# Retrieval feed-forward, state-space stage and eight-head context attention of a decoder joined into one block

## The reference

```
# L2 feed-forward: retrieval of experts beside a dense MLP
q = (x @ Wq.T).reshape(b, t, 2, 4, 64)             # two halves, 4 heads
sim = einsum('pbthn,hkpn->pbthk', q, keys)         # 128 keys
sx, ix = top_k(sim[0], 8); sy, iy = top_k(sim[1], 8)
scores, pk = top_k(all 64 sums of sx and sy, 8)    # per head
indices = ix * 128 + iy at pk                      # beyond 4095: the last row
w = silu(einsum(x, down_embed[indices])) * softmax(scores)
out = (silu(x @ Wg.T) * (x @ Wu.T)) @ Wd.T + einsum(w, up_embed[indices])
# L3 first part: state-space stage
u, v = split(x @ in_proj_w + in_proj_b); v = dwconv3(silu(v))
h[t] = a * h[t-1] + ssm_b * v[t];  y = ssm_c * h + ssm_d * v
out = layernorm((u * silu(y)) @ out_proj_w + out_proj_b + x) * ln_w + ln_b
# L3 second part: 8 heads of 64 over the context
out = softmax(q @ k.T / 8) @ v @ Wo + bo
```

## Time and profile before

| what | us |
|---|---|
| median of 3 runs | 3112.78 |
| lowest and highest run | 3108.11, 3117.63 |
| profiled execution, span from first to last instruction | 3106.5 |
| PE busy | 2320.2 (75%) |
| DVE busy | 1607.0 (52%) |
| ACT busy | 963.3 (31%) |
| POOL busy | 787.0 (25%) |
| mean granted clock of PE, share of full | 0.885 |

### The profile page before, as it was taken

How to read it: one execution, slowest core, us unless ns; L and a number is a source line. 1 busy time by engine, 2 the same in 40 slices (tenths; PEclk the granted TensorE clock), 3 DMA queues, 4 the chain that set the end, 5 groups by cost and what they waited for, 6 DMA issues and landing times. The chain is left out here.

```text
span 3106.5 us, 37880 instructions
## 1 busy us (share of the span) xinstructions
PE 2320.2 (75%) x13729; PEld 1493.0 (48%) x13729; DVE 1607.0 (52%) x4352; ACT 963.3 (31%) x1784; POOL 787.0 (25%) x755
## 2 busy tenths in 40 slices
PE   6877699888777655485677674877777877689786
PEld 3544378735443432462244333666666664237332
DVE  3754300067545657246374666655665544533486
ACT  0132222210241322132114463443334334424343
POOL 1000200041001006451000004777777771000000
PEclk9999699989998877796899897988889889899898
DMA  7200244337006142553500106222222221000000
GB/s 183 63 21 2 99 149 172 143 85 177 11 18 176 38 159 108 182 179 128 94 5 23 69 1 152 66 55 56 53 55 58 62 53 37 0 29 1 1 0 27
DMA packets 126828, 232.20 MB, mean 75 GB/s; under 512 B 38777, under 2 KB 76537, under 8 KB 122560
## 3 DMA queue, kind: packets, MB, share of 16 engines
q1 hardware_dynamic: 73552, 125.12, 14.2%
q0 software_dynamic: 51952, 100.65, 11.0%
q10 hardware_dynamic: 1152, 4.19, 0.3%
HBM read 245.59 MB, written 66.72 MB: 101 GB/s over the span
## 5 line engine op out<-in xcount | busy, mean ns | idle before, releaser
L3192 POOL DMA_INDIRECT L2f_G<-in_L2f_table,L2f_idx x512 | 523.7, 1023 | 288.7 <-issue 155.2
L3249 PE MATMUL psum<-L2f_G,L2f_diag 128*128 128x256 f32 x1024 | 304.4, 463 | 168.8 <-ACT L2f_diag L3319 168.8
L3249 PEld LDWEIGHTS psum<-L2f_G,L2f_diag 128*128 128x128 f32 x1024 | 235.9, 236 | 234.8 <-ACT L2f_diag L3319 192.0
L3427 DVE CUSTOM_DVE_ANT_0 L2f_junk<-L2f_G,L2f_X 128x256 bf16<-128x256 f32 x512 | 182.8, 421 | 254.0 <-DMA L2f_G<-in_L2f_table,L2f_idx 253.9
L3319 ACT ACTIVATE L2f_diag<-const,L2f_actd 128x128 f32<-128x128 f32 x528 | 161.1, 388 | 24.2 <-DVE L2f_actd L3441 24.2
L1191 PE MATMUL psum<-constb 128*128 128x256 bf16 x512 | 81.0, 282 | 96.8 <-ACT L1a_PT L1358 24.6
L2669 POOL DMA_INDIRECT picks_x<-L1f_rows,L1f_put x64 | 71.0, 1109 | 242.1 <-ACT L1f_rows L2759 223.2
L3226 PE MATMUL psum<-xT,L2f_mw 128*128 128x256 f32 x512 | 123.2, 385 | 0.0
L3312 ACT ACTIVATE L2f_actd<-L2f_dots 128x9 f32<-128x9 f32 (+1 forms) x64 | 13.5, 211 | 316.3 <-DVE L2f_dots L3427 316.3
L1358 ACT ACTIVATE L1a_PT<-psum 128x1536 f32<-128x1536 f32 x32 | 46.4, 1450 | 205.5 <-PE psum L1326 205.5
L1191 PEld LDWEIGHTS psum<-constb 128*128 128x128 bf16 x512 | 41.0, 99 | 142.2 <-ACT L1a_PT L1358 32.9
(11 more groups left out here) (689 smaller groups left out, 4882.8 us busy)
## 6 DMA issues: line engine op xcount, KB each, us to landing
L1f_we<-in_L1f_w SPq DMA_DIRECT2D x32, 384.0 KB, 8.2
picks_x<-zeros SPq DMA_DIRECT2D x16, 544.0 KB, 9.1
L1f_xe<-picks_x SPq DMA_DIRECT2D x32, 272.0 KB, 2.9
picks_y<-zeros SPq DMA_DIRECT2D x16, 512.0 KB, 6.4
L2f_G<-in_L2f_table,L2f_idx POOLq DMA_INDIRECT x512, 2.8
slots_x<-zeros POOLq DMA_DIRECT2D x8, 512.0 KB, 7.6
L1f_wb<-in_L2x_w SPq DMA_DIRECT2D x1, 4096.0 KB, 12.2
L1f_g<-picks_y ACTq DMA_DIRECT2D x8, 512.0 KB, 11.9
```

The source lines that it names most:

```text
L3192: nc.gpsimd.indirect_dma_start(out=G[:, h, k, :], out_offset=None, in_=ins["L2f_table"], in_offset=bass.IndirectOffsetOnAxis(ap=IDX[:, t, ...
L3249: mm = nc.tensor.matmul(ps[:, MIX_BANK + t % 2, 0:D], diag[:, i % 2, k, :], row[:, D:2 * D], start=(h == 0 and k == 0), stop=(h == HEADS - ...
L3427: e = V.tensor_tensor_reduce(out=junk[:, k, :], in0=row[:, 0:D], in1=X[:, t % 3, :], scale=1.0, scalar=0.0, op0=ALU.mult, op1=ALU.add, acc ...
```

## The change

Three stages become one block, `peer_tail_stage`. Batch m (256 tokens) goes through the state-space part in the eight steps after its last gather step, and through the context attention in the eight after those. The loop has 81 steps: 64 with gathers and 17 behind them. Chunks of the dense part become 256 tokens, so that a batch is complete after 8 steps. Each of the three parts gets PSUM banks of its own, and so one bank for `up` and one for the picks. The gathered rows lie in a ring of 28. The three normalizations are done a batch at a time, and no table set is named for ACT in this block. L3x's weights are laid in the free columns of both weight buffers. L3f's weights come in two loads once the gather steps are over. A few index instructions of DVE are merged.

```diff
+    CW = SEQ
+    PER = STEPS // B
+    LATER = 2 * PER + 1
+    END = LATER + PER * (B - 1) + PER
+    ROWS = 28
+    MIX, SIM, UP, DOWN, SSM, SSM2, CROSS, CROSS2 = range(8)
+        def ssm_at(i):
+            m, d = divmod(i - PER - 1, PER)
+            return (m, d) if 0 <= m < B else (0, None)
+        def cross_at(i, part):
+            m, e = divmod(i - LATER, PER)
+            return (m, 2 * e + part) if 0 <= m < B else (0, None)
...
+                        if n >= ROWS and (k == 0 or (n - ROWS) % TOPK == 0):
+                            pool.wait_ge(s["pk_used"].sem, s["pk_used"].at((n - ROWS) // TOPK + 1))
+                        nc.gpsimd.indirect_dma_start(
+                            out=G[:, n % ROWS, :], out_offset=None, in_=ins["L2f_table"],
...
@@ PE
-                    if i + 1 < STEPS:
-                        up(i + 1)
-                    if h == 0 and t + 2 < NT:
-                        queries(t + 2)
-                    picks(i)
-                    if i:
-                        down(i - 1)
+                    cross(i, 0)
+                    if h == 0 and 0 < t <= NT:
+                        turn_back(t - 1)
+                    if i < STEPS:
+                        if h == 1 and t + 2 < NT:
+                            pe.wait_ge(s["pk_hid"].sem, s["pk_hid"].at(i + 1))
+                            pe.wait_ge(s["pk_yadd"].sem, s["pk_yadd"].at(t))
+                            similar(t + 2)
+                        if h == 2 and t + 3 < NT:
+                            pe.wait_ge(s["pk_hid"].sem, s["pk_hid"].at(i + 1))
+                            queries(t + 3)
+                    ssm(i)
+                    if i < STEPS:
+                        picks(i)
+                    cross(i, 1)
+                    if i < STEPS:
+                        pe.wait_ge(s["pk_hid"].sem, s["pk_hid"].at(i + 1))
+                        down(i)
...
+                        if i + 1 < STEPS:
+                            up(i + 1)
@@ ACT
+                def inverse_root(bank, root, square, done):
+                    link(nc.scalar.activation(root, ps[:, bank, 0:CW], ACT.Ln, bias=c.eps))
+                    link(nc.scalar.activation(root, root, ACT.Exp, scale=-0.5))
+                    nc.scalar.activation(square, root, ACT.Square).then_inc(s[done].sem, 1)
...
+                    if h == 0 and 0 < t <= NT:
+                        keep(t - 1)
+                    if i < STEPS:
+                        weigh(i)
+                        diagonal(i)
+                    cross(i, 0)
...
+                    ssm(i)
+                    cross(i, 1)
+                    if i < STEPS and h == 3 and t + 2 < NT:
+                        exps(t + 2)
                     if i + 1 < STEPS:
                         gate(i + 1)
@@ DVE
-                    dot(i)
...
-                    gated(i)
-                    weighted(i)
+                    if i < STEPS:
+                        gated(i)
+                    ssm_gate(i)
+                    if i < STEPS:
+                        dot(i)
+                    late = cross_at(i, 0)[1] == 10
+                    if not late:
+                        cross(i, 0)
+                    if i < STEPS:
+                        weighted(i)
...
+                    ssm(i)
+                    if i < STEPS:
+                        if h == 2 and t + 2 < NT:
+                            best_keys(t + 2)
+                        if h == 3 and t + 2 < NT:
+                            best_pairs(t + 2)
+                        if h == 0 and 0 < t < NT - 1:
+                            experts(t + 1)
+                        if i == 1:
+                            prepare()
+                    cross(i, 1)
```

More of the change, by code:

```diff
@@ L82 @@
 }
+ROUTE_N, SSM_N, CROSS_N = PACK["L2f"][1], PACK["L3a"][1], 2 * 2 * 512
+LAST_N = PACK["L3f"][0]["w2"][0]
+CROSS_PLACE = {k: (0, ROUTE_N + a, n) if a < CROSS_N else (1, SSM_N + a - CROSS_N, n) for k, (a, n) in PACK["L3x"][0].items()}
+WIDTHS = (max(PACK["L3f"][1], ROUTE_N + CROSS_N), max(SSM_N + PACK["L3x"][1] - CROSS_N, PACK["L1a"][1], PACK["L1f"][1]))
 CONST, CONST_N = columns(("ident", P), ("mean", P), ("cos", SEQ), ("sin", SEQ), ("eps", 1), ("blank", 16))
@@ L1809, in fixed_ffn_stage @@
         with nc.Block() as block:
-            @block.sync
-            def _(sp):
-                c.prefetch(sp, name)
             @block.gpsimd
@@ L3214, in similar @@
                         for half in range(2):
-                            rows = slice(half * RD, (half + 1) * RD)
-                            mm = nc.tensor.matmul(ps[:, SIM_BANK + half, tile(o_)], q[rows, o_, :],
-                                                  w["keys"][rows, o_ * KEYS:(o_ + 1) * KEYS], start=True, stop=True)
+                            part = slice(half * RD, (half + 1) * RD)
+                            mm = mm_(ps[:, SIM + half, tile(o_)], q[part, o_, :],
+                                     w["keys"][part, o_ * KEYS:(o_ + 1) * KEYS], start=True, stop=True)
@@ L3255, in turn_back, with average @@
                     for j in range(DH):
-                        mm = nc.tensor.transpose(ps[:, MIX_BANK + t % 2, tile(j)], mix[:, 0, tile(j)], c.ident)
+                        mm = nc.tensor.transpose(ps[:, SIM, tile(j)], mix[:, tile(j)], c.ident)
                     mm.then_inc(s["pk_yturn"].sem, 1)
-                c.wait_weights(pe, name)
+                def average(bank, y):
+                    for j in range(DH):
+                        mm = mm_(ps[:, bank, 0:CW], c.mean, y[:, j, :], start=(j == 0), stop=(j == DH - 1))
+                    return mm
@@ L3260, in _ @@
+                c.wait_weights(pe, "L2f")
                 for t in range(2):
@@ L3328, in _ @@
+                c.wait_weights(act, "L3a")
+                nc.scalar.activation(decay[:, :], wa["la"], ACT.Sigmoid).then_inc(s["decay"].sem, 1)
                 for t in range(2):
@@ L3458, in _ @@
                     experts(t)
-                for i in range(STEPS):
+                for i in range(END):
                     t, h = divmod(i, HEADS)
-                    dot(i)
-                    if h == 1 and t:
+                    if i < STEPS:
[8 more added lines that the diff above has]
+                        weighted(i)
+                    if late:
+                        cross(i, 0)
+                    if h == 0 and 0 < t <= NT:
                         add_mix(t - 1)
@@ L3479, in peer_stage @@
         s["even_landed"].base += 16
-        work.close()
-        norm_stage(nc, c, name, acc)
-OTHER = {"L2f": peer_stage, "L1f": moe_top4_stage, "L2x": bitnet_stage, "L0f": moe_top1_stage, "L3f": fixed_ffn_stage, "L3a": ssm_stage}
+OTHER = {"L2f": peer_tail_stage, "L1f": moe_top4_stage, "L2x": bitnet_stage, "L0f": moe_top1_stage, "L3f": fixed_ffn_stage}
 def program(nc, ins, out):
@@ L3518, in program @@
         run = STAGES
-        packed = [n for n in run if n in PACK]
+        packed = [n for n in STAGES if n in PACK and n != "L3f"] + ["L3a"]
         c.w, order = {}, {}
```

966 lines of the change are left out of this document (438 added, 528 removed).

## The result

The changed kernel takes 3329.31 us (median of 4 runs, 3315.74 to 3331.43) against 3114.17 (3108.11 to 3117.63): ratio 1.068, 95% interval 1.066 to 1.071. It is slower by 215 us; the forecast was 3286 with a range of 3185 to 3370. The profiled execution took 3331.43, its span 3329.5, where the earlier trace rows has 3106.5.

A forecast was written before the change was run, and what follows sets the result against it. Gathers on POOL bound the old stage; the new order closes a ring. First picks, query tile, steps (117.6, 123.2, 822.5), tail 109 and end make 1222.3 against 1049.1, 173 more: 3280 span, 3286 us forecast, range 3185 to 3370.

The forecast's parts named there:

- The bound of before: Old retrieval feed-forward: POOL bound it, gathers back to back, one every 1.33 us, 10.6 us per step of eight.
- the closed ring: Gather steps: dots, diagonals, picks, down, up, silu, product wait in a circle, without overlap of the next step; 13.9 us.
- The bare step: Gather step without state-space or attention work, steps 1 to 8: 14.7 us.
- rival B: Lower TensorE clock on all picks: 147 us at most, some 100 to 110 more, 3390 us; chance 0.11.
- The exps of a tile's fourth step: Two table loads around the softmax exp, between picks and next silu in each fourth step, cost some 0.3 us on average.
- The slots: Added state-space and attention work, eight slots each: together 23.1 us per eight steps, 2.9 a step, making 17.5 us.
- the turning point: Mean gather step below which joining the stages pays: 14.1 us, with the bare ring at 13.4 to 14.7.
- Table loads: ScalarE in the joined block: two loads for each Ln with its Exp, some 160 loads in all.
- Rival A: One table load for Ln and Exp, 48 pairs of 1.28 us: 61 us less, 3225 us; chance 0.14.
- The tail: 17 steps after the last gather step: state-space chain about 40, woven attention 28, last attention 41; sum 109 us.
- The last attention's 41: Final attention running alone at the block's end, from Q projection through output and normalization: 41 us.
- Rival C: Gather steps not set by the ring but by the larger of POOL's and PE's work: 124 us less, 2989; chance 0.04.

The follow-up runs named there:

- experiment 1: Changed kernel with the table set holding both Ln and Exp asked for by name on ScalarE: 3271.08 us, ratio 1.051 to the kernel before.
- Experiment 8: Changed kernel with dots ahead of the product, Ln/Exp table set named, up projection ahead of picks in half the steps: 3094.48 us, 0.994.
- experiment 9: Experiment 8 plus four useless TensorE products before the picks in the two middle steps of each tile: 3113.88 us, 1.000.
- 11: Experiment 8 plus four useless TensorE products after each piece of attention work in the 17 steps behind the last gather step: 3102.72 us, 0.997.

## Why the forecast was right, and where its sizes were off

- **The bound of before and the closed ring: right.** Gathers back to back are gone, the ring's five waits show, and opening it by one order on DVE takes 145 us off.
- **The bare step: right but for the picks.** Over steps 1 to 8 the time between two groups of picks is 9.45 us, and the forecast has 9.14 + 0.16 + 0.3 = 9.6. The picks take 6.02 where it has 4.76 + 0.3. So the term "PE idles longer ahead of its picks, for which I add 0.3" is the whole miss of 0.8: it should have been 1.25. Some 0.15 of that are the ninth row's two passes, which the sum has on DVE and ACT but not on PE; the rest is the clock. Over all steps the picks take 5.43 against 4.86 before. That is rival B in part. Against it I had read in the earlier trace rows that the level comes back within one group; it does, but in the bare steps PE idled 3.4 to 6.7 us right before each group, and 6.02 lies two thirds of the way from 3.53 (all passes at 2.4 GHz) to 7.06 (all at 1.2). Filled, the step is 13.69.
- **The exps of a tile's fourth step: 0.3 where nothing was due in bare steps.** The two loads and the Exp run beside the picks (1974.74 to 1981.43 in this step), and the next silu waits for the up projection, not for them:

```profile
1974.71 1.28 ACT L3059 ACT_TABLE_LOAD   x1
1976.00 0.23 ACT L3059 ACTIVATE L2f_sc<-L2f_sc 128x32 f32<-128x32 f32 x1
1976.25 1.28 ACT L3065 ACT_TABLE_LOAD   x1
1984.06 0.39 ACT L3065 ACTIVATE L2f_h<-psum 128x256 f32<-128x256 f32 x1 [6.53 <-PE psum L2861]
```

  The first steps of a tile, which follow them, take 15.6 and 15.5 us, as the others do (15.46 on average).
- **The slots: right in sum, less so one by one.** The work of slot d ends in the interval of the step after it. Forecast against measured, slots 0 to 7: 19.0/18.6, 16.9/15.7, 17.8/20.0, 16.2/16.5, 16.5/15.6, 21.6/22.2, 17.1/18.7, 15.6/15.1. "A slot of 21 in every eight" is the sixth one at 22.2. The means are 17.5 and 17.8. Over 63 steps all these terms miss by 25 us (8 x 0.76, 8 x 0.67, 47 x 0.29). Two small slips are in the sum itself: slot 1 has 10.8 - 8.4 = 2.4 where it says 2.2, and the turning point's 13.4 at full clock still holds the 0.3 that stands for the clock.
- **Table loads: right.** 165, on the path nearly everywhere (0.92 us back for each one removed). Rival A fell on the two loads per pair. What it would have been is near experiment 1: 3271 with 63 loads fewer, some 3285 (an estimate) with the 48 of the pairs alone at 0.92 each. I had worked out 3225, from a base 43 too low and with 1.28 for each load.
- **The tail: mis-sized, 109 against 130.4.** The last attention's 41 is not the sum of the terms that stand there. They give 24.4 as listed and 35.1 with those of a unit taken twice, and the rest can only be the loads "in places". From its Q projection to the end of the block it took 46.4, so 41 was not far off. But my sum for the last attention began with its Q projection. The keys and values of that batch come before it, behind the normalization of the batch before:

```profile
3096.72 5.56 PE L2939 MATMUL psum<-cT,weights 128*128 128x120 f32 x16 [4.48 <-DVE xT L3287]
3102.21 4.05 PE L2943 MATMUL psum<-weights,cT 128*120 128x512 f32 x4
3107.09 5.43 PE L2952 MATMUL psum<-xT,weights 128*128 128x256 f32 x16 [0.83 <-issue]
```

  This is 10.4 us left out. Q took 5.43 instead of 3.4 and the output 5.4 instead of 3.4 (clock 0.78 in the tail), some 4 more; the rest, some 6, lies in the woven part ahead, and was not tested by itself.
- **Rival C and the turning point: the condition was right.** I put it at a mean step under 14.1 us. Experiment 8 gets 10.10, 11.77 and 14.85, mean 13.9, and with a tail of 110.7 it is just faster than before. It needed three changes to the order and the loads, not the joining alone. Rival C's step at POOL's pace comes true only in steps 1 to 8.

What stays open: whether the steps from 17 on are now bound by ACT's order in all slots (in experiment 8 the product waits 92.6 us for ACT, and ACT 209.9 for the dots); no kernel moved the attention's work to other slots.

## What to carry to other kernels

Before later work is put into the idle time of a loop, follow one step around all engines in the new program order: if each engine's first wait is for the end of the one before it, in a circle, the loop's time is the sum of them all, and the idle time that one meant to fill is created by the move. Compare that sum with the loop's old bound first; look for the one order (here the dots ahead of the product) that lets two steps overlap. Weave in functions that need different tables only with the set named, and count the loads wherever ACT is on the path: of the 1.28 us of each, 0.92 came back here on average and 1.08 in the tail.

## What the runs showed of the hardware

- TensorE's passes took longer when it had waited before them: the same 16 took 6.28 us after 4.58 us idle, and 3.72 after 0.93 idle behind other work. 259.5 us of useless products made the kernel 46 us faster. Where they stood in front of needed passes, the kernel lost (experiments 9 and 11: 19 and 8 us), in the latter although the clock rose to 1.00.
- With work added into TensorE's idle time the granted clock rose, over the span 0.856 to 0.896 and 0.842 to 0.900, in the tail 0.83 to 1.00; in experiment 9, with little idle time left, it did not (0.884 and 0.881).
- The automatic choice of a table set takes a load for Ln and another for the Exp right behind it, 48 times out of 48; by name there is one.
